# Reordering the last work items of an expert layer: third and fourth quarter of the last tiles interleaved, the fourth quarter's weight splits given to the first nine tiles

## The reference, cut to what matters

```python
x = layernorm(x + attention(x))                     # 4 sequences of 256 tokens
x = layernorm(x + gated_mlp(x, expert by token id)) # 4 experts, their matrices from ctx
x = layernorm(x + moe(x))                           # the step of this change

# moe: top 1 of 4 experts, by softmax(x @ Wr + br)
g = x @ Wg[e]                # 256 -> 1024
u = x @ Wu[e]                # 256 -> 1024
y = (silu(g) * u) @ Wd[e]    # 1024 -> 256
out = y * top_weight
```

## Time and profile before

| | |
|---|---|
| median of 3 runs | 210.68 us |
| the profiled execution's own time | 211.95 us |
| its span, first to last instruction | 210.2 us |
| TensorE busy | 180.8 us |
| VectorE busy | 131.8 us |
| GpSimd busy | 112.6 us |
| ScalarE busy | 98.8 us |
| mean granted TensorE clock, of full speed | 0.95 |

### The profile page before, as it was taken

One profiled execution on the slowest core, in us unless ns is written; L12 is line 12 of the kernel. 1 busy time (PEld: TensorE's weight loads), 2 busy tenths in 40 slices (PEclk: granted clock), 3 DMA queues, 4 the chain that ended last, 5 costly groups with the idle time before them and its releaser, 6 DMA issues.

```text
span 210.2 us, 3907 instructions
## 1 busy us (share of the span) xinstructions
PE 180.8 (86%) x979; PEld 143.9 (68%) x979; DVE 131.8 (63%) x407; ACT 98.8 (47%) x254; POOL 112.6 (54%) x140
## 2 busy tenths in 40 slices
PE   1999988989691988589899999999999999999910
PEld 0877767656470875157688887888888888888710
DVE  4279977517742568765466537455489996888850
ACT  2157768044331462335566485664366632344530
POOL 6033467799003347674387506885068850266783
PEclk9999999799998599799999999999999999999985
DMA  5999921359999103134445430545304000011010
GB/s 159 347 363 420 364 78 56 116 158 303 342 338 408 51 26 108 31 89 107 111 154 161 153 138 0 154 150 168 134 2 153 0 0 3 0 42 62 20 58 22
DMA packets 15301, 29.14 MB, mean 139 GB/s; under 512 B 1710, under 2 KB 11952, under 8 KB 15154
## 3 DMA queue, kind: packets, MB, share of 16 engines
q1 hardware_dynamic: 13552, 25.68, 36.8%
q0 software_dynamic: 1440, 3.22, 4.3%
q10 hardware_dynamic: 290, 0.01, 0.1%
HBM read 20.41 MB, written 9.28 MB: 141 GB/s over the span
## 4 chain that ended last, share of the span: by engine, by line
PE 58%; POOL 12%; DMA 11%; issue 8%; DVE 5%; SPq 2%; ACT 1%; POOLq 1%; DVEq 0%; ACTq 0%
PE bank L464 13%; PE bank L466 12%; PE bank L465 12%; DMA x_sorted<-padrow 8%; POOL out_tokens L453 5%; PE bank L702 4%; PE bank L529 3%; POOL rstd L382 3%; PE bank L478 2%; PE bank L560 2%; PE bank L538 2%; DMA arena<-in_xT 2%; POOL rstd L414 2%; SPq L294 2%; POOL x_sorted L426 1%
## 5 line engine op out<-in xcount | busy, mean ns | idle before, releaser
L378 POOL TENSOR_TENSOR w_lo<-stage,w_hi 128x512 fp32r<-128x512 f32 x48 | 61.2, 1300 | 44.9 <-ACT w_hi L773 44.9
L864 ACT ACTIVATE gate<-bank 128x256 f32<-128x256 f32 x44 | 17.0, 387 | 48.5 <-PE bank L466 45.2
L1165 DVE TENSOR_TENSOR hid<-bank,gate 128x256 f32<-128x256 f32 x44 | 18.7, 424 | 30.5 <-ACT gate L864 30.2
L464 PE MATMUL bank<-w_hi,xr 128*128 x88 | 35.8, 407 | 1.9 <-DVE xr L1129 1.7
L466 PE MATMUL bank<-w_hi,xr 128*128 x88 | 34.8, 395 | 0.0
L465 PE MATMUL bank<-w_lo,xr 128*128 x88 | 34.7, 394 | 0.0
L464 PE MATMUL bank<-w_hi,hT 128*128 x88 | 28.5, 324 | 0.7 <-DVE hT L1170 0.7
L773 ACT ACTIVATE w_hi<-stage 128x512 fp32r<-128x512 f32 x48 | 28.6, 630 | 0.3 <-PE bank L466 0.3
L466 PE MATMUL bank<-w_hi,hT 128*128 x88 | 24.9, 283 | 0.0
L465 PE MATMUL bank<-w_lo,hT 128*128 x88 | 24.8, 282 | 0.0
L464 PEld LDWEIGHTS bank<-w_hi,xr 128*128 128x128 f32 x88 | 16.7, 189 | 4.9 <-issue 2.8
(11 more groups left out here) (176 smaller groups left out, 329.8 us busy)
## 6 DMA issues: line engine op xcount, KB each, us to landing
stage<-in_w_ffn SPq DMA_DIRECT2D x16, 768.0 KB, 4.7
x_sorted<-padrow SPq DMA_DIRECT2D x1, 4356.0 KB, 17.0
rows<-x_sorted SPq DMA_DIRECT2D x22, 132.0 KB, 2.2
buf<-in_x_tok SPq DMA_DIRECT2D x1, 1024.0 KB, 10.9
w_hi<-in_ctx SPq DMA_DIRECT2D x1, 1024.0 KB, 11.5
w_hi<-in_ctxT SPq DMA_DIRECT2D x1, 1024.0 KB, 14.0
x_sorted<-padrow SPq DMA_DIRECT2D x1, 792.0 KB, 12.6
arena<-in_xT SPq DMA_DIRECT2D x1, 768.0 KB, 6.7
```

The costliest lines, as they stand in the source:

```text
L378: g.tensor_tensor(out=lo, in0=src, in1=hi.bitcast(F32), op=ALU.subtract).then_inc(split_lo, 1)
L464: mm(dst, xhi, whi, start=start, stop=False)
L864: a(gate[:, (T + j) % 2, :], fA[j % 2][:, 0:FQ], ACT.Silu).then_inc(silu_done, 1)
L1165: v.tensor_tensor(out=hid[:, (T + j) % 2, :], in0=fA[j % 2][:, FQ:2 * FQ], in1=gate[:, (T + j) % 2, :], op=ALU.mult).then_inc(h_done, 1)
```

## The change

The list of items gets another order at its end. Before, quarter 2 of all eleven tiles came ahead of quarter 3 of all eleven. Now it is: quarter 2 of tiles 0 to 8, quarter 3 of tiles 0 to 7, then (2, 9), (3, 8), (3, 9), (2, 10), (3, 10). The first item of quarter 3 is the 32nd of the list (index 31) instead of the 34th (index 33). The number of items and what each does stays the same.

All splits of quarter 3 have to come ahead of it, so that quarter has its own share list: tile 6 has 2 pieces instead of 1, and tile 9 has none instead of 1. The last piece is now split beside tile 8 (index 30). The rest follows from the order: `finish`, `finish_norm` and `norm_row` go by whether the item that they are due for is one of quarter 3, and look up its index.

```diff
-        share = [0, 1, 1, 2, 1, 2, 1, 2, 1, 1, 0]
+        SHARES = [None, [0, 1, 1, 2, 1, 2, 1, 2, 1, 1, 0], [0, 1, 1, 2, 1, 2, 1, 2, 1, 1, 0],
+                  [0, 1, 1, 2, 1, 2, 2, 2, 1, 0, 0]]
         def quarter_pieces(q, t):
+            share = SHARES[q]
             a = q * Q_PIECES + sum(share[:t])
             return range(a, a + share[t])
-        items = [(q, t) for q in range(NQ) for t in range(T)]
+        items = [(q, t) for q in range(NQ - 1) for t in range(T - 2 if q == NQ - 2 else T)]
+        items += [(NQ - 1, t) for t in range(T - 3)]
+        items += [(NQ - 2, T - 2), (NQ - 1, T - 3), (NQ - 1, T - 2), (NQ - 2, T - 1), (NQ - 1, T - 1)]
+        at_item = {item: j for j, item in enumerate(items)}
...
-                t = i - 4 - (len(items) - T)
-                if t >= 0:
-                    norm_row(t)
+                if i >= 4 and items[i - 4][0] == NQ - 1:
+                    norm_row(items[i - 4][1])
...
             def finish(t):
-                dve.wait_ge(y_done, T + len(items) - T + t + 1)
+                j = at_item[NQ - 1, t]
+                dve.wait_ge(y_done, T + j + 1)
...
-                dve.wait_ge(y_read, len(items) + t + 1)
+                dve.wait_ge(y_read, T + j + 1)
...
-                if 2 <= i <= len(items) + 1 - T:
+                if 2 <= i <= len(items) + 1 and items[i - 2][0] < NQ - 1:
                     fsum(i - 2)
...
-                if i - 2 >= 3 * T and i - 2 < len(items):
-                    finish(i - 2 - 3 * T)
-                if i - 3 >= 3 * T:
-                    finish_norm(i - 3 - 3 * T)
+                if 2 <= i <= len(items) + 1 and items[i - 2][0] == NQ - 1:
+                    finish(items[i - 2][1])
+                if i >= 3 and items[i - 3][0] == NQ - 1:
+                    finish_norm(items[i - 3][1])
```

More of the change, by code:

```diff
@@ L253, in route_kernel @@
         assert sum(ACT_SPLITS) == sum(POOL_SPLITS) == Q_PIECES
-        share = [0, 1, 1, 2, 1, 2, 1, 2, 1, 1, 0]
-        assert sum(share) == Q_PIECES and len(share) == T
+        SHARES = [None, [0, 1, 1, 2, 1, 2, 1, 2, 1, 1, 0], [0, 1, 1, 2, 1, 2, 1, 2, 1, 1, 0],
+                  [0, 1, 1, 2, 1, 2, 2, 2, 1, 0, 0]]
+        assert all(sum(share) == Q_PIECES and len(share) == T for share in SHARES[1:])
         def quarter_pieces(q, t):
+            share = SHARES[q]
             a = q * Q_PIECES + sum(share[:t])
@@ L262, in route_kernel @@
         CONSTS = 22
-        items = [(q, t) for q in range(NQ) for t in range(T)]
+        items = [(q, t) for q in range(NQ - 1) for t in range(T - 2 if q == NQ - 2 else T)]
+        items += [(NQ - 1, t) for t in range(T - 3)]
+        items += [(NQ - 2, T - 2), (NQ - 1, T - 3), (NQ - 1, T - 2), (NQ - 2, T - 1), (NQ - 1, T - 1)]
+        assert sorted(items) == [(q, t) for q in range(NQ) for t in range(T)]
+        at_item = {item: j for j, item in enumerate(items)}
         block = ctx.enter_context(nc.Block())
@@ L1192, in finish @@
             def finish(t):
-                dve.wait_ge(y_done, T + len(items) - T + t + 1)
+                j = at_item[NQ - 1, t]
+                dve.wait_ge(y_done, T + j + 1)
                 r = buf[:, t, 0:D]
-                v.scalar_tensor_tensor(out=r, in0=fY[(len(items) - T + t) % 2][:, 0:D], scalar=topw[:, t:t + 1],
+                v.scalar_tensor_tensor(out=r, in0=fY[j % 2][:, 0:D], scalar=topw[:, t:t + 1],
                                        in1=acc[:, t, :], op0=ALU.mult, op1=ALU.add).then_inc(y_read, 1)
-                dve.wait_ge(y_read, len(items) + t + 1)
+                dve.wait_ge(y_read, T + j + 1)
                 step(v.bn_stats(stats[:, t % 2, :], r))
```

## The result

The changed kernel took 213.84 us in the median of 20 runs (212.54 to 217.71), the kernel before 211.13 us in the median of its 20 (209.97 to 264.46). The ratio is 1.0112 with a 95% interval of 1.0092 to 1.0132. Every ratio in this document leaves out the runs that were more than 1.5% above the fastest of their kernel, here six of the changed kernel at 216.4 to 217.7 us and the 264.46 of before. By the medians of all runs the change costs 2.7 us, by the ratio 2.4. The forecast was 214.0 us.

The account below looks back on a forecast made before the run. TensorE, running without a gap, was taken as the bound (58% of the chain). Stall +3.4, clock +1.4 and tail -1.4 made +3.4 us; applied to the median of 210.68 us, the forecast was 214.0 us, range 212.3 to 215.4.

Parts of the forecast that it names:

- Step 1: TensorE's wait for the splits before item 31: GpSimd's seven pieces end late, stall +3.4 us (3.0 to 4.5).
- Step 2: VectorE's residual instruction beside denser splits: up to 0.3 us late an item, hidden by the stall, cost 0.
- Step 3: TensorE's clock around the stall: it falls to 0.50 for about 3.3 us, +1.4 us (0 to 1.9).
- Step 4: Last tile's way out: its root no longer waits behind an output on GpSimd, -1.4 us (-1.5 to 0).
- The clock stays up: Rival, TensorE at the stall: no fall of the clock, +2.0 us, 212.7 us; chance 0.19.
- The full lock: Rival, GpSimd's low parts: held up for VectorE's whole instruction, stall 4.5 us, 215.2 us; chance 0.12.
- The tail doesn't gain: Rival, after the last matmul: GpSimd or ScalarE late for another reason, +4.8 us, 215.5 us; chance 0.07.
- Not slower: Rival, wait at item 31: pieces nearly in time, stall 1.4 us or less, 209.3 us without any; chance 0.03.

Follow-up runs that it names:

- after_again: The changed kernel, unaltered, measured once more: median 216.53 us (6 runs), ratio 1.0223 to the kernel before.
- the experiment in which the cover is gone: The kernel before with its old item order and only the new share list (tile 6 two pieces, tile 9 none): ratio 1.007, median 212.18 us.
- one_moved_early: The changed kernel with only (2, 10) moved, between (3, 9) and (3, 10), and the fourth quarter's pieces given out earlier: ratio 1.0013 to the kernel before.
- the experiment with a gap of 0.85 us: The changed kernel with the last two low parts of the fourth quarter computed for one column of 512 only: ratio 0.9956.

## Why the prediction was right

**The level and the change.** That 213.84 us lie so near the forecast of 214.0 is partly luck. The forecast set out from 210.68, the median of three runs; that of twenty is 211.13. It forecast a change of +3.3 us, and 2.7 were measured by the medians, 2.4 by the ratio. The signs and the mechanisms of the four steps were right, the sum somewhat too high.

**Step 1, the wait: mechanism right, size 0.4 us too high.** 3.4 us were forecast with a lower bound of 3.0; it was 2.97, just under that bound. Two terms are off. The contention: I put one encounter into each of four residual instructions and added 0.3 us to the rate of the triples. But an encounter makes VectorE itself late (2.68 us an item), so fewer fit into the run, and the last one (166.51 to 167.98) has no low part behind it that it could lengthen; seven pieces took 9.31 us (9.29 in after_again), which is the triples' rate with nothing added. Against 8.82 without any encounter, contention is about 0.5 us in the run. The start: 0.24 us taken from the earlier trace rows, 0.14 measured.

**Step 2, VectorE: right here, its price wrong.** In the changed kernel it costs nothing, since TensorE waits in front of item 31 and VectorE catches up meanwhile. "If that weren't there, up to 0.3 us" failed: the experiment in which the cover is gone cost 0.69, and in one_moved_early 1.4 us.

**Step 3, the clock: right that it falls, its range too narrow.** 1.4 us forecast, 1.61 in the profiled execution, but 2.80 in another one, beyond the upper bound of 1.9. I took the length of the fall from the one example that I quoted (3.3 us), although the clock of before was low at another place for longer (from 66.4 to 73.2, after 4.5 us of idle time). The fall itself was less certain than one example made it look. The idle time of about 2.2 us that the earlier trace rows shows stands in all thirteen profiled executions of this document, between 80.9 and 87.0 us. In nine of them the clock fell to 0.50 at most 1.4 us after its end, for 3.4 to 10.2 us; in four it did not. One of the four is the changed kernel's second execution (after_again); its idle time, and the stretch behind it:

```profile
83.80:85.90 2.10, 0.00 (x0) 0.00 (x0) 1.38 (x11) 0.82 (x2) 1.24 (x4) 1.00 0.18 64
85.90:89.90 4.00, 2.54 (x17) 1.10 (x18) 2.65 (x16) 1.37 (x3) 2.75 (x6) 1.00 0.20 59
```

So a gap of that length gives no sure fall. At the longer gap of the changed kernel it came in both profiled executions, which is too few to call it certain.

**Step 4, the tail: right.** 1.4 forecast, 1.41 measured, and by the mechanism named: the last root waits for its variance and no longer for an output.

**The sum** was 3.4 us against 3.17 in the first pair of traces: half of the stall's 0.4 too much was taken back by the clock's 0.2 too little. Between these 3.17 us and the 2.4 to 2.7 of the timed runs 0.5 to 0.8 remain. They aren't explained: executions also differ ahead of item 30, and how many of the timed ones had which fall of the clock isn't known.

**The rivals.** "The clock stays up" is not what the two profiled executions of the changed kernel show; that it never does so in a timed run isn't shown. The full lock failed on GpSimd's side: the Trainium skill, page "SBUF — State Buffer", section "SBUF: two separate sides", says that the one that comes second blocks for the whole instruction of the other. VectorE does (1.54 against 0.48 us): its long instructions stay open until the low part that was running has ended, and 0.3 us more. GpSimd lost 0.49 us in seven pieces, where full blocking by 0.48 at each of three meetings inside the run would be 1.4. "The tail doesn't gain" is refuted by its 3.68 us. "Not slower" would have needed a gap under 1.4 us; the experiment with a gap of 0.85 us is on that side, at a ratio of 0.9956 (0.9916 to 0.9996).

## What to carry to other kernels

When a step is moved ahead, follow what it waits for back to the engine that prepares it, and compare the microseconds by which the step moves (here 4.66, two items) with those by which the preparation moves (here 1.3, with 0.5 of slack before). Ask of a reordering which single move brings the gain: one item between the last two tiles gave all of the tail's 1.4 us, and the preparation had room for that item without a stall once its pieces were given out early. (Two items with such a list weren't tried.) Work that must come sooner belongs where the preparing engine is idle early, not packed into an unbroken run just ahead of the deadline.

## What the runs showed of the hardware

- In dense matmuls, TensorE's idle time of 2.8 us (the gap of 2.97) was followed by a fall of the clock to 0.50 in both profiled executions, once for some 3.4 us and once for some 6.8; 1.74 us of idle time (the gap of 1.90) were not, in the one profiled execution. Idle time of about 2.2 us earlier in the program was followed by a fall in nine of thirteen executions. With twelve 512-column products in the gap the clock stayed at 1.00, in both profiled executions.
- VectorE's residual instruction, which reads two tiles in SBUF, lasts up to 1.54 us instead of 0.48 while GpSimd works through 128 x 512 subtractions, and costs GpSimd about 0.2 us each time (1.44 to 1.48 us instead of 1.28). The victim is VectorE, and through it TensorE, not the splits.
